# Projecting the values too ahead of the down product, with split operands stored during the up product and another preparation of the weights

## The chip, the core and the metric

The kernel runs on one core of a Trainium2 chip. The metric is the device time of the whole program in microseconds (us). Five engines run their own instruction queues: TensorE (PE: matmuls and transposes; PEld is its weight load), VectorE (DVE), ScalarE (ACT), GpSimd (POOL) and SyncE (SP), which here issues most DMA transfers. They meet only at semaphores.

## The reference

Four residual layers over x (32 sequences of 128 tokens, 256 features), all float32:

```python
x = x + L0_xattn(layernorm(x), ctx, ctx, mask)   # 16 heads of 16, no weights
x = x + L0_ffn(layernorm(x))                     # below
x = x + L1_xattn(layernorm(x), ctx, ctx)         # 16 heads of 64; q, k, v = x@Wq+bq, ctx@Wk+bk, ctx@Wv+bv
                                                 # softmax(q k / 8) v @ Wo + bo + query, then a layer norm
x = x + L1_ffn(layernorm(x))                     # route to the best of 8 experts of 1024; all experts'
                                                 # biases (relu(b1) @ W2 + b2) act on every token
# L0_ffn; qdq rounds to 16 bits by the maximum of the whole tensor, w_* to 4 bits by blocks of 32
x = qdq(x); up = qdq(x @ w_up.T); gate = qdq(x @ w_gate.T)       # 256 -> 768
o = qdq(qdq(gate * qdq_u16(sigmoid(gate))) * up); return o @ w_down.T
```

## The kernel before

Four functions, each a block with a queue written by hand for every engine, run one after another. Names of tiles begin with a_, b_, c_ and d_ after the function. `NB` is 32 sequences, `NC` 8 chunks of `CH` = 512 tokens, `NF` 6 and `ND` 2 blocks of 128 features. Products that need full precision are made of two parts of each operand: a rounded one (`high`, on ScalarE) and the difference (`low`, on VectorE or GpSimd); three of the four products of parts are summed (`PARTS`), so a block of 128x512 outputs from 256 features takes six matmuls.

`attention0` takes a step per sequence. Ahead of step 0, `weight_quantiser` brings all three weight matrices of the first feed forward through VectorE (six instructions each), TensorE (36 transposes in all) and ScalarE, and `statistics` makes the layer norm statistics of eight sequences; the others follow in steps 0 to 2, eight at a time. A block of its own before it loads the identity.

`feed_forward0` finds the maximum of y with GpSimd's all-reduce (`scale_of`, also for the maxima of up, gate, silu and inner), makes the up product and the gate product (`chunk`: 36 matmuls; ScalarE's `copy_chunk` empties the six banks of a chunk; VectorE's `quantise_up` rounds a chunk of up, and the copies of the gate product write over it), and then sigmoid and silu in 12 units of 2048 columns. Beside these, TensorE projects the keys of the second attention for all contexts: 64 blocks (`key_block`), contexts loaded by SP, rounded by ScalarE (`round_context`), their differences made on GpSimd (`split_context`), each block copied by ScalarE (`copy_keys`, three output buffers) and stored by SP (`store_keys`, 256 KB) in `keys_scratch`. `idle_sums` multiplies relu(b1) by the experts' second weights in 16 pieces, four loads of 128 KB each. SP issues these in one written order. Then `round_weights` and `rest_of_weights` split the down weights, and the down product follows with `low_inner`, the residual and the next layer norm's statistics.

`attention1` projects queries two sequences ahead and values too: `values(b, u, j)` on TensorE (12 matmuls a step), `copy_values` on VectorE with the bias bv added, and `round_context` and `split_context` for every second sequence. Keys come from `keys_scratch`, 1 MB for two sequences. Within a step the four groups of heads go: scores (PE, L1501), maxima (DVE, L1650), exponentials (ACT, L1798), division (DVE, L1661), transposes, copy, weighted values. The order on VectorE ends so:

```python
divide(b, 2)
copy_values(b, u, 0)
divide(b, 3)
add_residual(b - 1, (u + 1) % 2)
copy_values(b, u, 1)
```

`experts` sorts the tokens by expert, in tiles of 128 slots: VectorE builds which slot each token has, TensorE turns that into ids, GpSimd gathers the rows. Meanwhile GpSimd sums the experts' constants (L2075 to L2082), and VectorE makes of them what each expert's token lacks (`other`, L2340).

## Time and profile before

| | |
|---|---|
| time, median of 3 runs | 1593.12 us (1592.54 to 1595.28) |
| the profiled execution | 1594.02 us, span 1592.3 us |
| mean granted TensorE clock | 0.937 of full speed |
| busy PE, DVE, ACT, POOL | 1351.9, 1226.0, 1014.9, 435.5 us |
| moved by DMA | 134.54 MB, 84 GB/s over the span |
| attention 0, feed forward, attention 1, experts | 0 to 302, to 690, to 1281, to 1592 us |

The busy times say how much an engine did, not whether it set the pace; idle time of an engine that others wait for is what counts. DMA share is the mean busy share of the core's 16 DMA engines.

### The profile page before, as it was taken

How to read it: one execution, taken by the hardware profiler on the slowest of the kernel's cores; microseconds unless marked ns; L12 is line 12 of the kernel's file. 1: busy time of each engine (PE TensorE's matmuls, PEld its weight loads, DVE VectorE, ACT ScalarE, POOL GpSimd, SP SyncE). 2: the span in 40 equal slices, each digit the busy share in tenths (PEclk: the TensorE clock that was granted, in tenths of full speed). 3: DMA queues.
4: the chain of work that ended last, by engine and by line, in shares of the span. 5: the costliest groups of instructions: out<-in, count | busy, mean ns of one | idle time of the engine just before them, and what ended most of it. 6: DMA issues, size and time to landing. Idle time of an engine off the chain costs nothing. (4 is left out here: it accounts for less than half of the span.)

```text
span 1592.3 us, 35348 instructions
## 1 busy us (share of the span) xinstructions
PE 1351.9 (85%) x11195; PEld 1151.3 (72%) x11195; DVE 1226.0 (77%) x2165; ACT 1014.9 (64%) x2689; POOL 435.5 (27%) x663
## 2 busy tenths in 40 slices
PE   2688888599957797959999999999999729999996
PEld 2355555488833577958888888788888628999996
DVE  5777777667869788746888777777888677888886
ACT  2577888555567686626666665666666507888885
POOL 2434333100010120030222222222322243444553
PEclk8899999799978898979999999999999859999999
DMA  6511111000037364460221211131121047311110
GB/s 192 160 34 35 36 33 37 15 1 0 0 114 250 113 217 147 125 225 2 83 72 63 71 59 59 63 98 64 59 69 55 21 181 295 126 46 54 51 46 10
DMA packets 89827, 134.54 MB, mean 84 GB/s; under 512 B 11267, under 2 KB 74766, under 8 KB 84881
## 3 DMA queue, kind: packets, MB, share of 16 engines
q1 hardware_dynamic: 84752, 120.91, 22.9%
q0 software_dynamic: 4992, 12.60, 2.6%
q8 instruction: 44, 0.72, 0.2%
q14 instruction: 39, 0.31, 0.1%
HBM read 97.54 MB, written 38.67 MB: 86 GB/s over the span
## 5 line engine op out<-in xcount | busy, mean ns | idle before, releaser
L1798 ACT ACTIVATE c_w_raw<-c_ps_score,c_shift 128x128 f32<-128x128 f32 x512 | 183.7, 393 | 161.6 <-DVE c_shift L1653 153.0
L2182 PE MATMUL d_ps_hT<-d_zT,d_w_tile 128*128 128x128 f32 x1248 | 148.0, 277 | 2.3 <-DVE d_zT L2287 2.3
L2182 PEld LDWEIGHTS d_ps_hT<-d_zT,d_w_tile 128*128 128x128 f32 x1248 | 144.8, 194 | 2.9 <-DVE d_zT L2287 2.9
L2355 ACT ACTIVATE d_h<-d_ps_hT,d_b1T 128x128 f32<-128x128 f32 x312 | 88.4, 366 | 59.9 <-PE d_ps_hT L2182 59.9
L487 DVE TENSOR_REDUCE a_row_max<-a_ps_score 128x8 f32<-128x1024 f32 x64 | 78.0, 1219 | 58.5 <-PE a_ps_score L398 58.5
L2195 PE MATMUL d_ps_y<-d_w_parts,d_hT 128*128 128x256 f32 x936 | 121.5, 286 | 1.8 <-DVE d_res L2318 1.8
L1798 ACT ACTIVATION_READ_ACCUMULATOR c_w_raw<-c_ps_score,c_shift 128x1 f32 x512 | 119.0, 232 | 0.0
L1531 PE MATMUL c_ps_proj<-c_xnT,c_wq 128*128 128x256 f32 x768 | 110.1, 295 | 7.9 <-DVE c_v L1667 6.9
L2195 PEld LDWEIGHTS d_ps_y<-d_w_parts,d_hT 128*128 128x128 f32 x936 | 114.3, 191 | 2.0 <-DVE d_res L2318 2.0
L2306 DVE TENSOR_TENSOR d_w_parts<-d_w,d_w_parts 128x1024 fp32r<-128x1024 f32 x78 | 95.3, 1222 | 24.0 <-ACT d_w_parts L2367 23.1
L1554 PE MATMUL c_ps_proj<-c_wv,c_ctxT 128*128 128x512 f32 x384 | 106.3, 413 | 6.5 <-ACT c_qT L1820 3.3
L580 ACT ACTIVATE a_probT<-a_ps_probT 128x512 f32<-128x512 f32 x128 | 71.3, 625 | 57.2 <-PE a_ps_probT L409 57.2
L1531 PEld LDWEIGHTS c_ps_proj<-c_xnT,c_wq 128*128 128x128 f32 x768 | 98.4, 195 | 12.4 <-DVE c_v L1667 7.4
L1476 POOL TENSOR_TENSOR c_var_o<-c_mv_o,c_eps 128x1 f32<-128x1 f32 x32 | 6.7, 211 | 355.9 <-DVE c_mv_o L1711 355.9
L1594 PE MATMUL c_ps_aux<-c_wo,c_attnT 128*128 128x256 f32 x768 | 101.4, 288 | 1.7 <-DVE c_attnT L1686 1.7
L1594 PEld LDWEIGHTS c_ps_aux<-c_wo,c_attnT 128*128 128x128 f32 x768 | 95.6, 192 | 2.0 <-issue 1.9
L957 ACT ACTIVATE b_act<-b_ps 128x512 f32 (+1 forms) x96 | 56.6, 598 | 63.1 <-PE b_ps L876 58.4
L1661 DVE TENSOR_TENSOR c_w_raw<-c_w_raw,c_inv_sum 128x512 f32<-128x512 f32 x128 | 88.7, 693 | 4.4
L2367 ACT ACTIVATE d_w_parts<-d_w 128x1024 fp32r x78 | 79.8, 1051 | 17.0 <-PE d_ps_y L2195 16.8
L1650 DVE TENSOR_REDUCE c_row_max<-c_ps_score 128x4 f32<-128x512 f32 x128 | 87.3, 682 | 1.2 <-PE c_ps_score L1501 1.1
L1092 DVE TENSOR_REDUCE b_pmax<-b_act (+1 forms) x96 | 63.2, 683 | 32.2 <-ACT b_act L957 32.0
L1554 PEld LDWEIGHTS c_ps_proj<-c_wv,c_ctxT 128*128 128x128 f32 x384 | 68.9, 192 | 21.8 <-ACT c_qT L1820 5.9
(265 smaller groups left out, 3663.0 us busy)
## 6 DMA issues: line engine op xcount, KB each, us to landing
keys_scratch<-b_key_out SPq DMA_DIRECT2D x64, 256.0 KB, 2.5
c_kT<-keys_scratch SPq DMA_DIRECT2D x16, 1024.0 KB, 5.5
d_w<-w_in SPq DMA_DIRECT2D x16, 1024.0 KB, 10.3
b_x_space<-w_in SPq DMA_DIRECT2D x64, 128.0 KB, 2.8
zx_scratch<-c_zx SPq DMA_DIRECT2D x32, 256.0 KB, 2.3
a_x<-x_in SPq DMA_DIRECT2D x4, 1024.0 KB, 7.6
a_keys<-ctx_blocks_in SPq DMA_DIRECT2D x128, 32.0 KB, 2.1
a_v_raw<-ctx_in SPq DMA_DIRECT2D x4, 1024.0 KB, 8.5
```

Of the source, the lines that this page charges most:

```text
L487: dve.tensor_reduce(row_max[:, half, :], ps_score[:, half], AX_X, ALU.max).then_inc(max_done, 1)
L1531: last = pe.matmul(ps_proj[:, j, h * PT:(h + 1) * PT], weights[:, a, k, blk * P:(blk + 1) * P], src[:, c, k, :], start=(n == 0), stop=(n = ...
L1554: last = pe.matmul(ps_proj[:, j, :], ctxT[:, 1 - u // 2, a, k, tok], wv[:, c, k, j * BANK:(j + 1) * BANK], start=(n == 0), stop=(n == ND * ...
L1594: last = pe.matmul(ps_aux[:, 0:D], attnT[:, s, a, blk, :], wo[:, c, blk, :], start=(n == 0), stop=(n == BLKS * len(PARTS) - 1))
L1650: dve.tensor_reduce(row_max[:, n, :], ps_score[:, n % 2], AX_X, ALU.max).then_inc(max_done, 1)
L1661: dve.tensor_tensor(prob[:, n], prob[:, n], inv_sum[:, n, :].unsqueeze(2).to_broadcast([P, HB, P]), ALU.mult).then_inc(prob_ready, 1)
L1798: last = act.activation(prob[:, n, j, :], ps_score[:, n % 2, j, :], ACT.Exp, scale=float(KD) ** -0.5, bias=shift[:, n, j:j + 1], accum_out ...
L2182: last = pe.matmul(ps_hT[:, f, :], w1_tile[:, half, k, n * P:(n + 1) * P], zT[:, s, k, :], start=(k == 0), stop=(k == ND - 1))
L2195: last = pe.matmul(ps_y[:, 0:D], hT[:, s, a, f, :], w2_parts[:, half, b, n, :], start=(f == 0 and (a, b) == PARTS[0]), stop=(f == FB - 1 a ...
L2306: dve.tensor_tensor(w2_parts[:, half, 1], w2[:, e, half * FB // 2:(half + 1) * FB // 2, :], w2_parts[:, half, 0].bitcast(F32), ALU.subtrac ...
L2355: act.activation(h[:, f, :], ps_hT[:, f, :], ACT.Relu, bias=b1T[:, e, f:f + 1]).then_inc(h_ready, 1)
L2367: act.activation(w2_parts[:, half, 0], w2[:, e, half * FB // 2:(half + 1) * FB // 2, :], ACT.Copy)\
```

## The change

- *Opening.* `weight_quantiser` is gone. `attention0` loads x in parts of 2, 6, 8, 8 and 8 sequences, the identity within its block, and quantises w_up alone there; statistics go for sequences 0 and 1, 2 and 3, 4 to 7, and from then on one sequence ahead in each step (`statistics_ahead` on VectorE, `deviation_ahead` on GpSimd). w_up is turned in the last steps (12 transposes, 3 copies). Half of the first keys are loaded by ScalarE's queue.
- *The maximum of y* goes over TensorE (two transposes) and VectorE; GpSimd makes one all-reduce that nobody needs first.
- *During the up product* twelve items of 128x1024 are split: Wk in two halves, eight chunks of contexts, Wv in two halves. Each is loaded by SP, rounded by ScalarE, its difference made by VectorE, and both parts stored (1 MB) in `split_scratch`. The gate weights are quantised and turned there too. Before VectorE quantises up it waits for all these stores.
- *Before the down product* TensorE makes 64 key blocks and 64 value blocks. Their operands come ready from `split_scratch` by loads that GpSimd issues: 16 turns of eight blocks with 2 x 512 KB, and four loads of 1 MB for weights. Output buffers are five; pieces of `idle_sums` come after every third block, with one buffer; ScalarE copies four blocks after each unit of sigmoid and three after most units of silu. The down weights are quantised on VectorE among the last units and turned ahead of the last eight blocks. No engine starts the down product before all 128 blocks are done.
- *Attention 1* loads the values (512 KB for a sequence) from `values_scratch`; wv, `values`, `copy_values`, `round_context`, `split_context` are gone. bv is taken through Wo: eight matmuls of 128x256 and an addition to bo once, ahead of the steps.
- *Experts.* The constants' sums are eight matmuls and three copies on ScalarE; one of the wide VectorE instructions (`at_tile[:, :, 0]`) goes to ScalarE; the first gather is issued right after its own ids.

The diff, cut to its core:

```diff
+                load_x(0)
+                sp.dma_start(ident[:], eye).then_inc(ident_loaded, 16)
+                sp.dma_start(w_sb[:].rearrange("p (o i) -> p o i", i=D), w_up.rearrange("(o p) i -> p o i", p=P)).then_inc(w_loaded, 16)
+                load_mask(0)
+                load_first_keys(sp, 0, 0, range(0, HALF, 2))
+                load_x(1)
+                load_v(0)
+                load_first_keys(sp, 1, 1, range(HALF))
...
-                quantise_weights(dve)
-                statistics(0)
+                dve.wait_ge(x_loaded[0], 16)
+                statistics(0, 2)
+                quantise()
+                dve.wait_ge(x_loaded[1], 16)
+                statistics(2, 4)
...
+                def load_raw(k):
+                    if k >= 2:
+                        sp.wait_ge(split_ready, k - 1)
...
+                def store_split(k):
+                    sp.wait_ge(split_ready, k + 1)
+                    sp.dma_start(split_dram[k], split[:, k % 2].bitcast(F32)).then_inc(split_stored[k % 2], 16)
...
+                for n in range(ALL):
+                    store_block(n)
+                    if n % IDLE_EVERY == IDLE_EVERY - 1 and w2_pieces < 2 * FB:
+                        load_w2(w2_pieces)
+                        w2_pieces += 1
...
+                def load_contexts(first, end):
+                    for turn in range(first, end):
+                        if turn >= 2:
+                            pool.wait_ge(block_done, BLOCKS * (turn - 1))
+                        load_part(turn, 0)
+                        load_part(turn, 1)
...
+                pool.partition_all_reduce(one[:, 6, :], power[:, 0:1], P, bass.bass_isa.ReduceOp.max).then_inc(all_max, 1)
+                maximum(UP)
+                for s in range(2):
+                    pool.wait_ge(split_stored[s], 16 * ITEMS // 2)
+                load_part(0, 0)
+                pool.wait_ge(y_ready, 2 * NC)
+                load_half(WK, 0)
+                load_half(WK + 1, 1)
+                pool.wait_ge(product_done, (2 * NC - 1) * NF)
+                load_part(0, 1)
+                pool.wait_ge(product_done, 2 * NC * NF)
+                load_contexts(1, 2)
+                maximum(GATE)
+                load_contexts(2, 8)
+                maximum(SILU)
+                pool.wait_ge(block_done, KEYS - 4)
+                load_half(WV, 0)
+                load_contexts(8, 9)
+                pool.wait_ge(block_done, KEYS)
+                load_half(WV + 1, 1)
+                load_contexts(9, 14)
+                maximum(INNER)
+                load_contexts(14, 16)
...
+                def copy_block(n):
+                    act.wait_ge(block_done, n + 1)
+                    if n >= NO:
+                        act.wait_ge(block_stored[n % NO], 16 * (n // NO))
...
+                for u in range(NU):
+                    sigmoid(u)
+                    copy_blocks(done, done + 4)
+                    done += 4
...
                 scale_of(UP, pmax[:], factors[:, Y, 0, :])
                 by_gate[0] = 1
+                for s in range(2):
+                    dve.wait_ge(split_stored[s], 16 * ITEMS // 2)
                 quantise_up(0)
...
+                for u in range(NU):
+                    times_up(u, u % 2)
+                    if u >= 6:
+                        for step in range(2 * (u - 6), 2 * (u - 5)):
+                            quantise_down(step)
...
+                rest_of_weights(2, downT, down_parts)
+                dve.wait_ge(block_done, ALL)
...
+                def load_values(t, s):
+                    if inside(t, 4, NB - 1):
+                        sp.wait_ge(out_done, 2 * (t - 3))
+                    sp.dma_start(values[s].rearrange("p h w -> p (h w)"), values_dram[t]).then_inc(values_loaded[s], 16)
...
+                def bias_through_output():
+
+                    pe.wait_ge(w_loaded[1], 16)
+                    pe.wait_ge(bias_loaded, 16 * N_BIAS)
+                    for blk in range(BLKS):
+                        last = pe.matmul(ps_out[:, 0:2, :], bv[:, blk:blk + 1].to_broadcast([P, P]), w_raw[:, 1, blk * D:(blk + 1) * D],
+                                         start=(blk == 0), stop=(blk == BLKS - 1))
...
-                    if inside(b, *projects):
-                        copy_values(b, u, 0)
-                    if here:
                         divide(b, 3)
                     if back:
                         add_residual(b - 1, (u + 1) % 2)
-                    if inside(b, *projects):
-                        copy_values(b, u, 1)
...
-                pool.tensor_tensor(other[:], idle[:], b2[:], ALU.add).then_inc(summed, 1)
...
+                for e in range(NE):
+                    last = pe.matmul(sums[e], all_but[:, e:e + 1].to_broadcast([2 * NE, P]), constant_rows[:], start=True, stop=True)
```

## Rows read from the trace of the kernel before

**Rows 1.** Windows: busy us and count by engine, mean clock, DMA share, GB/s.

```profile
313.00:382.00 69.00, 69.00 (x286) 55.51 (x287) 46.76 (x61) 34.69 (x55) 0.00 (x0) 0.96 0.00 0
382.00:450.00 68.00, 67.90 (x291) 54.27 (x290) 54.04 (x69) 34.17 (x56) 0.35 (x1) 1.00 0.00 0
450.00:536.00 86.00, 53.67 (x272) 31.82 (x272) 78.12 (x43) 65.94 (x52) 14.15 (x5) 0.83 0.61 196
800.00:1200.00 400.00, 379.40 (x3412) 333.22 (x3414) 319.87 (x748) 256.64 (x1025) 104.79 (x184) 0.98 0.20 66
```

**Rows 2.** Timeline, ScalarE, first exponential of steps in attention 1: start, us, operation.

```profile
1033.93 0.42 ACT L1798 ACTIVATE c_w_raw<-c_ps_score,c_shift 128x128 f32<-128x128 f32 x1
...
1050.86 0.43 ACT L1798 ACTIVATE c_w_raw<-c_ps_score,c_shift 128x128 f32<-128x128 f32 x1
...
1068.51 0.42 ACT L1798 ACTIVATE c_w_raw<-c_ps_score,c_shift 128x128 f32<-128x128 f32 x1
...
1206.65 0.43 ACT L1798 ACTIVATE c_w_raw<-c_ps_score,c_shift 128x128 f32<-128x128 f32 x1
...
1222.20 0.43 ACT L1798 ACTIVATE c_w_raw<-c_ps_score,c_shift 128x128 f32<-128x128 f32 x1
...
1237.04 0.41 ACT L1798 ACTIVATE c_w_raw<-c_ps_score,c_shift 128x128 f32<-128x128 f32 x1
```

**Rows 3.** Timeline, VectorE, attention 0; in brackets the idle time before.

```profile
7.69 1.75 DVE L97 TENSOR_REDUCE a_w_scale<-yT 128x48 f32<-128x1536 f32 x1 [7.54 <-DMA yT<-w_up_in]
...
40.95 1.23 DVE L487 TENSOR_REDUCE a_row_max<-a_ps_score 128x8 f32<-128x1024 f32 x1 [9.01 <-PE a_ps_score L398]
...
80.86 1.23 DVE L487 TENSOR_REDUCE a_row_max<-a_ps_score 128x8 f32<-128x1024 f32 x1 [7.71 <-PE a_ps_score L398]
...
127.16 1.22 DVE L487 TENSOR_REDUCE a_row_max<-a_ps_score 128x8 f32<-128x1024 f32 x1 [1.50 <-PE a_ps_score L398]
```

**Rows 4.** Timeline, GpSimd, opening of the first feed forward.

```profile
308.40 0.38 POOL L851 PARTITION_ALL_REDUCE b_one<-b_one  x1 [5.60 <-issue]
```

**Rows 5.** Groups by line and shape, 450 to 608 us: busy, mean ns, idle before.

```profile
L1005 ACT ACTIVATE b_key_out<-b_ps,b_bk 128x512 f32<-128x512 f32 x63 | 40.6, 682 | 16.7 <-PE b_ps L901 8.4 <-DMA keys_scratch<-b_key_out 8.1
L1157 DVE SCALAR_TENSOR_TENSOR b_act<-b_act,yT 128x2048 f32<-128x2048 int32 x12 | 29.5, 2462 | 0.3 <-ACT b_act L980 0.3
...
L978 ACT ACTIVATE b_act<-yT,b_factors 128x2048 f32<-128x2048 int16 x12 | 24.0, 2000 | 4.9 <-DVE yT L1151 4.9
...
L891 PE MATMUL b_ps<-b_x_space,b_b1T 128*32 128x256 f32 x128 | 12.9, 482 | 22.5 <-DMA b_x_space<-w_in 22.5
L996 ACT ACTIVATE b_ctx_high<-b_ctx_raw 128x1024 fp32r<-128x1024 f32 x8 | 8.4, 1051 | 2.9 <-DMA b_ctx_raw<-ctx_t_in 2.9
```

**Rows 6.** Timeline, VectorE, first quantising of up.

```profile
386.96 5.28 DVE L1103 TENSOR_SCALAR b_up<-b_act,b_factors 128x3072 int16<-128x3072 f32 x3
```

**Rows 7.** DMA issues of the page: KB of each, us to landing.

```profile
keys_scratch<-b_key_out SPq DMA_DIRECT2D x64, 256.0 KB, 2.5
c_kT<-keys_scratch SPq DMA_DIRECT2D x16, 1024.0 KB, 5.5
```

**Rows 8.** Timeline, TensorE, first matmul of the down product.

```profile
616.28 0.55 PE L931 MATMUL b_ps<-b_down_high,b_inner 128*128 128x256 f32 x1 [8.43 <-DVE b_inner L1233]
```

**Rows 9.** Windows with much DMA traffic, columns as in rows 1.

```profile
500.00:505.00 5.00, 3.39 (x26) 1.60 (x25) 4.70 (x3) 4.97 (x5) 0.00 (x0) 1.00 0.83 254
1284.00:1296.00 12.00, 3.81 (x33) 3.33 (x33) 10.03 (x19) 0.00 (x0) 7.95 (x5) 0.64 1.00 418
```

**Rows 10.** Timeline, TensorE, opening of attention 1.

```profile
714.67 4.47 PE L1531 MATMUL c_ps_proj<-c_xnT,c_wq 128*128 128x256 f32 x24 [6.92 <-DVE c_v L1667]
```

**Rows 11.** Timeline, GpSimd and VectorE, opening of the experts.

```profile
1289.71 4.49 POOL L2075 TENSOR_TENSOR d_other<-d_idle,d_b 128x2048 f32<-128x2048 f32 x1 [3.97 <-DMA d_idle<-idle_scratch]
...
1289.80 4.44 DVE L2257 TENSOR_SCALAR d_slot_tile<-d_slot 128x32 int32<-128x32 int32 x1
...
1294.27 0.18 DVE L2258 TENSOR_SCALAR d_slot_row<-d_slot 128x32 int32<-128x32 int32 x1
```

880 lines of the change are left out of this document (498 added, 382 removed).

## Prediction, made before the change was run

> **What bounds the kernel now.** I read the page's slices first (TensorE busy nearly everywhere), then tables of windows by stage, then per stage the groups of lines and the timeline around each handover. The kernel is four blocks in a row, and what is last differs in each, so each part is costed in its own stage.
>
> [rows 1] show three regimes. In the two products of the first feed forward (313 to 450 us) TensorE is busy 69.0 of 69 and 67.9 of 68 us: only TensorE counts, and 291 matmuls of 512 columns in 67.9 us make 0.233 us each, thus 1.40 us for a block of six. From 450 to 536 it is busy 53.7 of 86 us: VectorE (78.1) and ScalarE (65.9) pace the stage, and the keys that TensorE projects there are its filler. In the second attention TensorE is busy 379 of 400 us, yet it isn't what sets a step: [rows 2] give the steps by their first exponential. Two neighbours take 16.93 and 17.65 us; the second is one that also splits a pair of contexts. Step 29 (1206.65) takes 15.55, step 30 (1222.20), which projects neither queries nor values, 14.84. Had TensorE set the step, the 12 value matmuls of 512 columns (2.8 us at 0.233) and the 24 of the queries less would have saved far more than 0.7. The step is a ring between ScalarE's exponentials and VectorE's maxima and divisions, and only a VectorE instruction inside that ring has a price.
>
> **The change, part by part**, against the profiled execution (1594.02, span 1592.3; the median of the runs, 1593.12, is 0.9 below it).
>
> *Opening of attention 0.* VectorE begins on the first weight matrix at 7.69 and takes the first row maximum at 40.95 [rows 3]: three matrices, statistics of eight sequences, and the turning of 36 pieces lie between. After, one matrix is quantised there: six instructions, three as wide as the first (1.75) and three lesser, which I estimate at 7 us together. Also, two sequences go first, and the identity's own block is gone, which I put at 1.5 us. I estimate load 5.5, statistics, quantiser to 12.5, two more sequences 1.1: first maximum near 14, so −27. The stall of 7.71 us at 80.86 (keys behind 3 MB of values and x) has the same cause and should stay, about 1 us shorter: −28. Bounds: −20 if keys or masks land late, −33 if that stall goes too. The per-step statistics (two instructions, 0.6 us) fit in VectorE's idle 1.50 us before each maximum [rows 3]; without that cover they would cost 24 × 0.6 = 14 us. Turning w_up in the tail: +1, since the tail waits for latencies and not for TensorE.
>
> *The maximum of y.* POOL's first all-reduce starts 5.60 us after it could [rows 4], with nothing that it waits for. It is replaced by two transposes and two short VectorE instructions (about 1.5 us in all), and a dummy all-reduce takes that delay aside: −4 (bounds −3 and −5).
>
> *During the up product.* Twelve items of 512 KB: a load, ScalarE's rounding 1.05 (the same tile in [rows 5]), VectorE's difference 1.23 (half of the 2.46 of a tile twice as wide there), a store of 1 MB; also gate's quantiser (7 us VectorE, 12 transposes, 3 copies). VectorE goes from 46.8 to 46.8 + 14.8 + 7 = 68 of 69 us, or to some 64 because the last items fall behind the product's end; ScalarE from 34.7 to about 50. The bytes, 18 MiB in 69 us, are 274 GB/s where now there are none. TensorE's work grows by some 1.5 us. The dear place is the end. VectorE waits for all split stores before it quantises up's first chunk. Before, that starts at 386.96 (5.28 for three, thus 1.8 each, [rows 6]); TensorE needs the first bank after six blocks from 382.5, thus at 391.0. After, the last two items are split at about 386.8, their stores land (a load of 1 MB took 5.5 us, [rows 7]) at about 393, VectorE 1.8, copy 0.6: 395.7, so TensorE stands about 4.5 us. With the transposes +5.5 (bounds 0, if the stores end early; +12, if the items drag behind).
>
> *From 450 to the first down matmul (616.28, [rows 8]): 166 us now.* After, TensorE does 128 blocks × 1.40 = 179, sixteen sums of pieces at 0.95 = 15 (four matmuls of 0.48 that overlap in part, and the gaps around them, [rows 5]), three groups of transposes 1.5: 195 us. It starts at once, for its first operands are loaded in the gate product. It replaces filler by work that bounds the stage: ScalarE has 128 copies × 0.68 = 87 and, for twelve units, three activations each of about the 2.00 of [rows 5], 72, in the same 195, VectorE the same as before plus 9 for the down weights; both fit. SILU's all-reduce no longer stops TensorE. But bytes: 32 MiB of blocks out, 16 MiB contexts, 4 weights and 8 w2 in, 62.9 MB. The w2 pieces all fall among the first 48 blocks: 12 + 6 + 2 + 8 MiB = 29.4 MB in what TensorE does in 82 us, 359 GB/s. Now this stage reached 254 GB/s at a DMA share of 0.83, 306 if full, while pure reads elsewhere reached 418 at 1.00 [rows 9]. By the nearer row, at about 325 GB/s, the first part takes 90 instead of 82: +8 (bounds 0 at 418, +14 at 306). The rest needs 302 GB/s: just about hidden. WV's load waits for block 60: +2. Then inner's rounding to the first down matmul, 3 us. Sum 195 + 8 + 2 + 3 = 208, so +42 (bounds +28: sums overlap and the DMA keeps up; +65: all at 272 GB/s). The down product's first matmul took 0.55 [rows 8], at the lower clock after 8 idle us; after 3 idle us it may keep the clock: −2 (bounds 0 and −3).
>
> *Opening of attention 1.* TensorE stands 6.92 us until VectorE has written values [rows 10], which is late through wo's 1 MB, its rounding and VectorE's 2.3 us. No wv, no context. But the new bias product also needs wo and all biases landed and adds 8 matmuls and an addition before the steps; the 512 KB broadcast of bv is gone. −7 (bounds −2 and −9).
>
> *Steps of attention 1.* Removed from VectorE's ring are the second value copy in 30 steps and the split of the context in 14. Step 29 against 30 prices the former at 0.71, neighbours in the loop the latter at 0.71 too [rows 2] (0.6 in the earlier steps). 30 × 0.71 + 14 × 0.63 = 30: −30. The first value copy and ScalarE's rounding of contexts lie in gaps. The 512 KB of values per step replace a 512 KB context in every second one; at 66 GB/s now [rows 1] that is free. Bounds −20 (the queries' new wait costs what the copy gave) and −58 (half way to TensorE's own time, D below).
>
> *Opening of the experts.* POOL's first sum holds 4.49 us, and a 128x32 VectorE instruction beside it takes 4.44 where the next of its size takes 0.18 [rows 11]. That delay (4.3), a smaller one beside the second sum and one of three wide VectorE instructions, which I estimate at 2.7 together, leave the path to the gather: −7 (bounds −4: the new matmuls at half clock hold the ids up; −8.5). The subtraction for the experts' biases was hidden behind the gather and is worth nothing.
>
> The sum: −28 + 1 − 4 + 5.5 + 42 − 2 − 7 − 30 − 7 = −29.5, so 1564.5 by the profile and 1564 by the median.
>
> **Rivals.** (A) *Slower: the block stores set the product stage.* ScalarE's copy n waits for store n − 5. Stores now land in 2.5 us [rows 7], but loads of 1 MB in 5.5. The stage must lose another 30 us, 0.23 a block, to undo all gains; blocks are 1.52 us apart with the sums, so that takes a store of about 5 × 1.75 = 8.8 us from copy to landing, or 265 GB/s on the whole. For it: loads of 512 KB and 1 MB beside every store, and 306 GB/s as the full share's rate [rows 9]. Against: even 306 gives 206 us for all bytes. At 250 GB/s the stage is 252 us: 1608.
> (B) *Slower too: POOL's context loads come late.* POOL issues them a turn (8 blocks, 11.2 us) ahead. In [rows 11] POOL and VectorE hold each other up. Should the two parts together wait more than 11.2 − 5.5 = 5.7 us, over two VectorE instructions of 2.46 [rows 5], TensorE stands; at 10 us a turn, 14 × 4.3 = 60: 1624. The Trainium skill (SBUF — State Buffer, "Who interferes with whom") says that descriptors of a DMA issued from GpSimd aren't written while VectorE runs in a two-port mode, and that this, not bandwidth, is what delays it. The rows of that group, [rows 11], agree that the two engines exclude each other for a whole instruction; no row here shows a load delayed so. Against B: one VectorE instruction per load is hidden.
> (C) *The splitting is not hidden in the up product.* VectorE at 68 of 69 and 274 GB/s leave no slack; with 10 to 20 us more, 1574 to 1584.
> (D) *TensorE sets the attention steps.* Its own time in a step is 0.949 × 17.3 = 16.4 us [rows 1], 13.6 without 2.8 for the values; some 26 steps × 3.6 give −94 in place of −30: 1500. Steps 29 and 30 speak against it.
> (E) *The product stage comes cheap* (+28, the DMA keeps up): 1550.
>
> **How the numbers follow.** Forecast as summed, with its own range 1555 to 1575: 0.50. E, or a like gain in attention 1: 0.20. D: 0.02. C: 0.13. A: 0.11, B: 0.04. Of A 0.03 and of C 0.01 end near the old time: faster 0.50 + 0.20 + 0.02 + 0.12 = 0.84, same 0.04, slower 0.08 + 0.04 = 0.12. What a measurement here can tell from no change is about 0.2%, 3.2 us. The range 1535 to 1590 leaves out D, and A and B in the main.
>
> **What would show it.** After, the first row maximum stands near 14 us, and the later stall stays; no 5.6 us gap ahead of the first up matmul; TensorE idle some 5 us early in the gate product; 207 us between the last gate matmul and the first down matmul, with a DMA share near 1 in its first half and TensorE above 0.9 busy; loop steps of 16.2 to 16.3 us of both parities; no VectorE instruction of 4.4 us among the experts' slots. The prediction is wrong above all if block stores show as what ScalarE waits for throughout, if TensorE waits for contexts at every eighth block, or if the steps keep their 17 us because the ring has a wait on TensorE that I haven't seen.

## The result

The change made the kernel slower: 1650.86 us, the median of four runs (1648.56 to 1655.41), against 1592.83 us before (1588.62 to 1595.28); the ratio is 1.0371, 95% interval 1.0338 to 1.0403. The forecast was 1564 with a range of 1535 to 1590, and faster than before. In the profiled executions the difference is 55.5 us of span (1647.8 against 1592.3).

Four lines of the trace after, one for each landmark: what a line's instructions did, with their count, their shortest, median and longest duration in ns, and when the first and the last began.

```profile
L995 PE MATMUL b_ps<-b_y_parts,b_gate_high x192: 390/393/767, 367.7 to 443.8; 128*128 128x512 f32 x192
...
L1089 PE MATMUL b_ps<-b_down_high,b_inner x384: 274/285/415, 703.9 to 774.4; 128*128 128x256 f32 x192
...
L1724 PE MATMUL c_ps_score<-c_kT,c_qT x1024: 271/272/580, 803.0 to 1318.9; 64*128 64x128 f32 x171
...
L2373 PE MATMUL d_ps_hT<-d_zT,d_w_tile x1248: 270/275/582, 1368.7 to 1628.0; 128*128 128x128 f32 x179
```

The same landmarks of the kernel before, from the same view, cut the time into pieces. Each piece is a difference of two starts:

| piece | before | after | change | forecast |
|---|---|---|---|---|
| start to the last row maximum of attention 0 | 288.7 | 277.0 | −11.7 | −28 |
| to the second chunk of the up product | 34.8 | 30.5 | −4.3 | −4 + 1 |
| to the end of the gate product | 125.8 | 136.3 | +10.5 | +5.5 |
| from there to the first down matmul | 167.0 | 260.1 | +93.1 | +42 |
| the down product | 71.6 | 70.5 | −1.1 | −2 |
| to the first scores of attention 1 | 34.2 | 28.6 | −5.6 | −7 |
| to its last scores | 533.4 | 515.9 | −17.5 | −30 |
| to the first tile of the experts | 58.8 | 49.8 | −9.0 | −7 |
| to the end | 278.0 | 279.1 | +1.1 | 0 |
| sum | | | +55.5 | −29.5 |

Of the 85 us between forecast and result, 51 lie in one piece, 16 in attention 0, 12 in the steps of attention 1 and 5 in the gate product. Windows of the trace after, to be read against [rows 1]: attention 0's loop, the 64 key blocks, the 64 value blocks, the loop of attention 1.

```profile
87.00:252.00 165.00, 134.78 (x1513) 89.53 (x1515) 129.89 (x240) 123.71 (x320) 73.29 (x159) 0.94 0.11 32
444.00:602.00 158.00, 114.65 (x514) 81.19 (x512) 81.82 (x54) 94.99 (x94) 11.15 (x19) 0.85 0.67 204
602.00:700.00 98.00, 93.24 (x396) 75.45 (x395) 54.45 (x39) 55.36 (x78) 8.33 (x16) 0.97 0.83 278
930.00:1267.00 337.00, 292.77 (x2712) 263.01 (x2712) 250.66 (x598) 217.47 (x880) 89.94 (x159) 0.91 0.29 93
```

The key half lasts 158 us with TensorE busy 115 of them and the DMA share at 0.67: neither engine nor bytes are at their limit. The value half, 98 us with TensorE busy 93, is close to the forecast. What the prediction priced at 90 us is the first 48 blocks with the sixteen sums; they took 133.2 us, with TensorE busy 90 of them:

```profile
444.30:577.50 133.20, 89.85 (x418) 61.31 (x416) 69.94 (x43) 78.12 (x74) 9.20 (x15) 0.84 0.70 210
```

In both loops the mean clock is below that of the kernel before: 0.94 in attention 0, where it was 1.00, and 0.91 in attention 1, where [rows 1] show 0.98.

What waited for what in the product stage, 445 to 690 us: engine, tile and line, what it waited for, us in total, times, longest.

```profile
ACT b_out L1173 <- PE b_ps L1043: 62.0, 30, 7.7
...
DVE b_act L1372 <- ACT b_act L1159: 61.5, 12, 12.9
...
PE b_ps L1018 <- DMA b_x_space<-w_in: 43.4, 10, 8.6
...
PE b_ps L1053 <- DMA b_ctx_low<-split_scratch: 4.8, 1, 4.8
...
ACT b_out L1173 <- DMA keys_scratch<-b_out: 4.6, 1, 4.6
```

TensorE waited 43.4 us for the pieces of the experts' weights, at ten of sixteen places; ScalarE and VectorE stood behind it. Of these, 4.4 us are the first piece, whose loads SP issues only after the gate product; the other 39 us are waits for a reload of the one buffer. The same wait stood already in the kernel before: 22.5 us, in the row of [rows 5] from which the prediction took the 0.48 us of these matmuls. There VectorE and ScalarE set the pace and TensorE had time to wait. For contexts it waited 4.8 us once, and ScalarE waited for key stores 4.6 us once: rivals A and B of the prediction are not what happened.

One turn of this wait in the timeline. TensorE:

```profile
489.46 0.40 PE L1043 MATMUL b_ps<-b_ctx_high,b_w_parts 128*128 128x512 f32 x1
496.52 1.08 PE L1018 MATMUL b_ps<-b_x_space,b_b1T 128*32 128x256 f32 x8 [6.66 <-DMA b_x_space<-w_in]
```

ScalarE at the same time:

```profile
487.73 2.00 ACT L1157 ACTIVATE b_act<-yT,b_factors 128x2048 f32<-128x2048 int16 x1
489.76 1.91 ACT L1159 ACTIVATE b_act<-b_act 128x2048 int32<-128x2048 f32 x1
491.58 1.25 ACT L1173 ACTIVATE b_out<-b_ps,b_bk 128x512 f32<-128x512 f32 x2
500.50 0.69 ACT L1173 ACTIVATE b_out<-b_ps,b_bk 128x512 f32<-128x512 f32 x1 [7.67 <-PE b_ps L1043]
```

and SyncE's DMA issues:

```profile
486.37 2.27 SPq L846 DMA_DIRECT2D b_x_space<-w_in  x3
489.16 1.12 SPq L853 DMA_DIRECT2D keys_scratch<-b_out  x1
497.66 1.78 SPq L846 DMA_DIRECT2D b_x_space<-w_in  x4
```

The buffer of the pieces is free once the sums before have run, at about 485.5 (they began at 484.89). SP issues the loads of the next piece from 486.37 to 489.1, since a block's store stands ahead of them, and ScalarE could copy that block only after the sigmoid that ended at 484.2. GpSimd issues two context loads of 512 KB at 487.41 and 487.95 beside them. TensorE has made its three blocks by 489.86 and gets the piece at 496.52. While it stands, no block is made; ScalarE, which comes out of the next sigmoid at 491.58, copies what there is and runs dry for 7.67 us until 500.50, so the next store and the next load (497.66) are late in turn. It is a ring of one buffer's release, SP's order behind ScalarE's copies, and a landing beside the contexts. From the first of a piece's four issues to the last arrival took 3.7 to 5.0 us for nine of the pieces and 7.1 to 10.1 us for the other seven; those seven overlap with GpSimd's loads of contexts, of the nine only one does for more than 1 us. The experiments take the first two links apart; no run moved the contexts' loads, so that link is seen in the traces and not tested.

The other places, each against its row of before. The opening of attention 0, where [rows 3] have 40.95:

```profile
8.82 1.75 DVE L533 TENSOR_REDUCE a_w_scale<-a_w 128x48 f32<-128x1536 f32 x1 [4.00 <-DMA a_w<-w_up_in]
...
17.90 1.19 DVE L459 TENSOR_REDUCE a_row_max<-a_ps_score 128x8 f32<-128x1024 f32 x1
```

The weights landed at 8.8 and not at 5.5; the first row maximum stands at 17.90 and not at 14. The opening of attention 1, where TensorE stood 6.92 us for VectorE [rows 10], now waits for the last bias:

```profile
790.96 2.47 PE L1819 MATMUL c_ps_out<-c_w_raw,c_bv 128*128 128x256 f32 x5 [4.06 <-DMA c_br<-br_in]
```

The experts' slots, where the first of these two took 4.44 us [rows 11]:

```profile
1352.70 0.18 DVE L2449 TENSOR_SCALAR d_slot_tile<-d_slot 128x32 int32<-128x32 int32 x1
...
1352.92 0.18 DVE L2450 TENSOR_SCALAR d_slot_row<-d_slot 128x32 int32<-128x32 int32 x1
```

### The profile page after: what moved, and what is told of

Its sections match the earlier page's. It is cut to its first block and busy times, and to the rows that moved or that the text cites. A ratio compares the mean times of both kernels' runs of the same rounds, so it can differ in the third digit from the quotient of the medians.

```text
span 1647.8 us, 35334 instructions
## 1 busy us (share of the span) xinstructions
PE 1389.3 (84%) x11229; PEld 1184.0 (72%) x11229; DVE 1183.1 (72%) x2102; ACT 1047.2 (64%) x2716; POOL 431.9 (26%) x735
## 5 line engine op out<-in xcount | busy, mean ns | idle before, releaser
L1754 PE MATMUL c_ps_proj<-c_xnT,c_wq 128*128 128x256 f32 x768 | 105.9, 288 | 0.0
L1724 PE MATMUL c_ps_score<-c_kT,c_qT 64*128 64x128 f32 x1024 | 92.6, 332 | 8.5 <-ACT c_w_raw L1996 6.9
L1754 PEld LDWEIGHTS c_ps_proj<-c_xnT,c_wq 128*128 128x128 f32 x768 | 94.4, 191 | 3.8 <-issue 0.2
L1724 PEld LDWEIGHTS c_ps_score<-c_kT,c_qT 64*128 64x128 f32 x1024 | 79.2, 232 | 24.8 <-ACT c_w_raw L1996 12.7
L1878 DVE RECIPROCAL c_inv_sum<-c_row_sum 128x4 f32<-128x4 f32 x128 | 22.4, 175 | 97.1 <-ACT c_w_raw L1996 97.1
L1043 PE MATMUL b_ps<-b_ctx_high,b_w_parts 128*128 128x512 f32 x256 | 91.9, 431 | 0.0
L2558 ACT ACTIVATE d_w_parts<-d_w 128x1024 fp32r x78 | 80.4, 1054 | 13.7 <-PE d_ps_y L2386 12.6
```

The lines of the kernel that those rows point to most:

```text
L1043: last = pe.matmul(ps[:, bank(n), :], w_parts[:, h, a, k, column:column + P], ctx_parts[c % 2][b][:, k, :], start=(j == 0), stop=(j == ND ...
L1724: last = pe.matmul(ps_score[:, r, j, :], qT[rows, s, blk, tok], kT[rows, s, blk, tok], start=True, stop=True)
L1754: last = pe.matmul(ps_proj[:, j, h * PT:(h + 1) * PT], weights[:, a, k, blk * P:(blk + 1) * P], src[:, c, k, :], start=(n == 0), stop=(n = ...
L2558: act.activation(w2_parts[:, half, 0], w2[:, e, half * FB // 2:(half + 1) * FB // 2, :], ACT.Copy)\
```

## Experiments

The first eleven ran once each beside one run of the kernel before (1594.44, 1592.55 and 1591.93 us in the three groups); what is said of them rests on pieces of their traces and not on a few us of the whole. How far such a piece scatters can be read from the runs in which its code is that of the change: the last row maximum of attention 0 came at 273.5 to 279.1 us (nine runs), the piece from the last gate matmul to the first down matmul took 257.8 to 266.5 us (six runs), first to last scores of attention 1 took 513.6 to 516.6 us (eleven runs).

### The product stage: who makes TensorE wait

**Loads three stores earlier in SP's order.**

```diff
                 for n in range(ALL):
+                    if (n + 3) % IDLE_EVERY == IDLE_EVERY - 1 and w2_pieces < 2 * FB:
+                        load_w2(w2_pieces)
+                        w2_pieces += 1
                     store_block(n)
-                    if n % IDLE_EVERY == IDLE_EVERY - 1 and w2_pieces < 2 * FB:
-                        load_w2(w2_pieces)
-                        w2_pieces += 1
```

> The changed kernel with one move in SP's written order: the loads of a piece of the experts' weights stand three block stores earlier, so that they wait only until TensorE has used the buffer and not also until ScalarE has copied the block before it. Same bytes, same buffers, same engine. Theory 1 (TensorE stands 43.4 us for these loads because SP reaches them late, behind stores whose copies ScalarE makes only after a sigmoid): the wait falls from 43.4 to about 15 to 20 us, the time from the last gate matmul to the first down matmul from 260 to about 230 us, the whole to about 1620. Theory 2 (the DMA engines are the limit of the key half): the same bytes take the same time, the wait moves to stores or contexts and the whole stays within 5 us of 1650.

1634.45 us. The wait fell to 30.0 us, the piece from the last gate matmul to the first down matmul from 260.1 to 243.6. The order in the queue is a third of the matter; I had expected more (a wait of 15 to 20 us, a piece of 230).

**The loads on GpSimd's queue.** `load_w2` moved there word for word, each released by TensorE's use of the buffer alone:

```diff
+                events = sorted([(IDLE_EVERY * i, 0, i) for i in range(1, 2 * FB)] + [(BLOCKS * (t - 1), 1, t) for t in range(2, 8)])
+                for _, kind, k in events:
+                    if kind == 0:
+                        load_w2(k)
+                    else:
+                        load_contexts(k, k + 1)
-                load_contexts(2, 8)
```

> The changed kernel with those loads issued by GpSimd's queue, each as soon as TensorE has used the buffer, merged by block number with the context loads that this queue already issues. Theory 1: as for the move in SP's order, 15 to 25 us of waiting left, whole about 1620 to 1630. Rival (loads issued by GpSimd are held back by VectorE's instructions): the wait stays at 40 us or grows, and the whole stays at 1650 or above, though the run with SP's earlier order gets faster.

1628.57 us, wait 25.6, piece 239.9 us. GpSimd's loads of 128 KB landed after 3.0 us (median), SP's in the other run after 2.8: VectorE doesn't hold them back by any amount that shows. What is left is 5.2 us for the first piece and 20.4 us that I put down to the single buffer: a load can start only when the last piece is used, and three blocks (4.2 us) don't cover the arrival of a piece, 4.2 to 8.3 us after its first issue in this run.

**Only one piece loaded.** All sums take the first piece, so the experts' constants come out of the wrong weights.

```diff
-                    if n % IDLE_EVERY == IDLE_EVERY - 1 and w2_pieces < 2 * FB:
-                        load_w2(w2_pieces)
-                        w2_pieces += 1
...
-                    pe.wait_ge(w2_loaded, 64 * (i + 1))
+                    if i == 0:
+                        pe.wait_ge(w2_loaded, 64)
```

> The changed kernel with only the first piece of the experts' weights loaded; all sixteen sums use it again, so the sums of the experts' constants are of the wrong weights, but TensorE does the same matmuls. It takes away 8 MB of loads and every wait for them. Theory 1: TensorE's 43.4 us of waiting are gone and most of it comes back: 1600 to 1610; the key half runs at ScalarE's pace (6.5 us for four blocks). Theory 2 (DMA bytes): 8 MB less at 250 GB/s is 33 us, about 1617, with the DMA share still above 0.85 through the key half; under theory 1 the share falls below 0.8.

1599.07 us, 51 us less than the change. Its two halves, and then its first 48 blocks with the sixteen sums:

```profile
444.00:552.00 108.00, 103.17 (x515) 74.65 (x513) 79.53 (x53) 90.16 (x90) 9.71 (x19) 0.98 0.71 219
552.00:654.00 102.00, 93.75 (x397) 75.86 (x398) 60.27 (x46) 61.32 (x85) 8.33 (x16) 0.97 0.85 282
...
444.40:529.50 85.10, 80.35 (x418) 56.42 (x416) 61.93 (x39) 70.04 (x68) 6.94 (x14) 0.98 0.71 216
```

The key half takes 107 us instead of 158. Of the 50 us between them about 39 are idle time of TensorE; the rest is its lower clock, for the same matmuls kept it busy 115 us at a mean clock of 0.85 in the change and 103 us at 0.98 here. The first part takes 85 us, where the prediction had 82 before it added anything for bytes: that estimate of TensorE's own work held. The whole piece is 210.0 us. It looks like the forecast 208, but 8 us of that sum were for the bytes of these loads, so 200 us are what to compare it with: 3 us more lie in the first part, 6 behind the sums. This run takes away the waits and 8 MB of loads together, so it doesn't say alone which of the two cost the 50 us; the DMA share of 0.67 in the change, and the next runs, which keep all bytes, do.

**Two buffers, three outputs.** The second buffer takes the space of two output buffers.

```diff
-        w2 = x_space[:, 0:4 * D].rearrange("p (e d) -> p e d", d=D)
+        w2 = x_space[:, 0:8 * D].rearrange("p (h e d) -> p h e d", h=2, d=D)
...
-                    if i >= 1:
-                        sp.wait_ge(idle_part, i)
+                    if i >= 2:
+                        sp.wait_ge(idle_part, i - 1)
```

> The changed kernel with two buffers for the pieces of the experts' weights, paid for with two of the five output buffers; SP's order as in the changed kernel but one piece ahead. Theory 1: the loads are a whole piece ahead, their wait falls below 5 us; three output buffers hold ScalarE's copies up by some us in all: whole 1605 to 1620. Rival A of the prediction (block stores set the pace): with three buffers instead of five the stage gets slower, over 1650, and ScalarE is seen to wait for stores for tens of us.

1633.02 us.

```profile
ACT b_out L1173 <- DMA keys_scratch<-b_out: 41.4, 19, 6.1
...
ACT b_out L1175 <- DMA values_scratch<-b_out: 39.4, 22, 5.8
...
PE b_ps L1018 <- DMA b_x_space<-w_in: 17.4, 6, 4.1
```

TensorE's wait for pieces fell to 17.4 (I had expected less than 5), but ScalarE now waits 81 us for its output buffers, and the value half takes 108 us. This is rival A's mechanism, brought about by three buffers; with five it stays at 17 us. The bound that I had set for it (a store must land 8.8 us late) was for five.

**Two buffers and five outputs.** The second buffer lies where the raw down weights were; these are loaded after the last sum.

```diff
-        w2 = x_space[:, 0:4 * D].rearrange("p (e d) -> p e d", d=D)
+        w2 = [flat[:, 0:4 * D].rearrange("p (e d) -> p e d", d=D) for flat in (x_space, downT[:].rearrange("p k n -> p (k n)"))]
```

> The changed kernel with two buffers for the pieces of the experts' weights and all five output buffers: the second buffer lies where the raw down weights lay, which are loaded after the last piece instead. The run with three output buffers lost its gain again to waits for stores, most of it in the value half (108 us instead of 93). Theory 1: with both, TensorE's wait for pieces stays below 10 us of 43, the value half is 93 us again, the first down matmul comes at 660 to 670 instead of 703.9, whole 1608 to 1618. Rival (bytes: 29.4 MB within the first 48 blocks at 235 to 250 GB/s are 118 to 125 us): the key half stays at 125 us or more, first down matmul at 672 or later, whole 1620 or more.

1618.1 us, piece 223.6: the wait for pieces is 14.7 us (8.0 and 6.7 for the two buffers), 5.1 of them for the first; the key half takes 122 us at a DMA share of 0.87 and 265 GB/s. With all bytes kept, 36 of the 50 us are back. Here the expectation's two theories meet: most of the ring's wait is gone, and what is left of the loss in the key half goes with the DMA's load; no run separates that rest further. The first 48 blocks take 99 us, still more than the 96 of the prediction's upper bound. The stores, too, now land after 5.2 us instead of 3.6.

**Pieces after every fifth block**, so that they reach into the value half:

```diff
-        IDLE_EVERY = 3
+        IDLE_EVERY = 5
...
-                copy_idle()
                 copy_blocks(done, done + 3)
...
+                    if u == 7:
+                        copy_idle()
```

> The run with two buffers for the experts' weights and five output buffers, with the pieces after every fifth block instead of every third, thus over 80 of the 128 blocks; the copy and the store of the sums, and the load of the down weights, come later by 32 blocks. Theory (in the key half the engines wait for latencies of a full DMA queue; the value half has room): the key half falls from 121 to 108 to 112 us, the value half grows by the six pieces that it gets (6 to 8 us), first down matmul at 662 to 668 instead of 669.8, whole 1611 to 1617. Rival (the down weights, which now come late, hold the end up): the time from the last value block to the first down matmul grows above 6 us, whole 1618 or more.

1605.27 us, better than the theory had it; piece 216.5.

```profile
446.00:560.00 114.00, 105.96 (x508) 77.89 (x507) 89.95 (x57) 93.44 (x93) 12.57 (x22) 0.97 0.96 300
560.00:665.00 105.00, 93.93 (x422) 74.30 (x421) 52.53 (x44) 58.47 (x83) 6.76 (x13) 0.96 0.80 264
```

The halves don't part where these windows do: the last key block ends at 548.0 and the first value block starts at 553.0. The key half is down to 102 us, the value half up to 106 (it holds four pieces, and VectorE waits 15.2 us for the sums' store before it may quantise the down weights).

### Attention 0: the step of 7.62 us

**Statistics in the first steps**, as before the change; the new opening stays.

```diff
                     if b == 0:
                         statistics(4, 8)
+                    else:
+                        dve.wait_ge(x_loaded[b + 1], 16)
+                        statistics(8 * b, 8 * b + 8)
...
-                        statistics_ahead(UN * i + u, u)
```

> The changed kernel, but with the layer norm statistics of the sequences 8 to 31 made eight at a time in steps 1 to 3 of attention 0, as the kernel before has them; nothing of them in the later steps, on VectorE or GpSimd. The new opening stays. Theory (the two statistics instructions per step outgrow VectorE's gap, which lengthens the step by 0.3 us, and TensorE, idle that much longer, is granted half its clock in every third step): the steps return to 7.62 us at a clock of 1.00; 24 steps of mean 8.3 become 7.62, minus 16 us, plus what the first steps take back, about 4: the last row maximum 12 to 13 us earlier than 277.0, whole 1637 to 1640. Rival (the new opening itself or the keys' queues slow all steps): steps stay at 7.9 and 9.5, whole 1650 or more.

Of the nineteen steps of the changed kernel from 86.5 to 245.0 us, five take 7.62 us and eight 7.9 at the full clock, and six take 9.5 at a mean of 0.82. Two of them that follow each other, cut at their first row maxima; in the second TensorE is busy 1.65 us longer with as many matmuls:

```profile
152.39:160.31 7.92, 6.30 (x77) 4.32 (x78) 6.63 (x12) 6.22 (x16) 3.71 (x9) 1.00 0.10 31
...
160.31:169.88 9.57, 7.95 (x77) 4.95 (x78) 6.65 (x12) 6.22 (x16) 5.28 (x12) 0.82 0.09 29
```

The run with the statistics first took 1641.67 us. The loop's steps are 7.62 us, the clock is 1.00, the last row maximum 12.6 us earlier:

```profile
87.00:252.00 165.00, 137.07 (x1664) 94.29 (x1656) 123.96 (x217) 132.01 (x349) 65.33 (x131) 1.00 0.12 35
```

**GpSimd's part alone left in the steps.** GpSimd makes the deviation ahead in every step from statistics that VectorE made early.

```diff
-                    pool.wait_ge(mv0_done, b + 5)
-                    pool.tensor_tensor(var_next[:, u:u + 1], mv_next[:, u, 1:2], eps[:], ALU.add)
+                    pool.wait_ge(mv0_done, NB)
+                    pool.tensor_tensor(var_next[:, u:u + 1], mv0[:, b + 4, 1:2], eps[:], ALU.add)
```

> As the run with the statistics in the first steps, but GpSimd still makes the deviation of one sequence ahead in each step. If VectorE's two instructions are the cause, the steps stay at 7.62 us with the clock at 1.00 and the whole equals that run's. If GpSimd's two instructions are (they hold shared work between the queries and the values), the steps stay at 7.9 and more, and the whole is 10 us or more above that run's.

1645.58 us, and the steps are 7.93 us again, some 9.5. The last row maximum comes 9.3 us later than in the run before; the whole is only 3.9 us longer, where I had expected 10 or more, since the product stage happened to take 4.7 us less. The theory that VectorE's instructions did it fell here: they are not in this kernel's steps. GpSimd's scaling of the next queries (L288) and VectorE's shift of the row maxima (L463), in this run:

```profile
150.30 0.61 POOL L288 TENSOR_TENSOR a_q_in<-a_q_in,a_rstd_next 128x256 f32<-128x256 f32 x1
...
150.33 0.61 DVE L463 TENSOR_SCALAR a_shift<-a_row_max 128x8 f32<-128x8 f32 x1
```

and in the run with the statistics first, in another step:

```profile
149.12 0.61 POOL L288 TENSOR_TENSOR a_q_in<-a_q_in,a_rstd 128x256 f32<-128x256 f32 x1 [0.17 <-POOL a_q_in L285]
...
149.89 0.17 DVE L463 TENSOR_SCALAR a_shift<-a_row_max 128x8 f32<-128x8 f32 x1
```

GpSimd's two new instructions push its L288 past 150.3, where VectorE's shift begins; the two start 30 ns apart, and 0.17 us become 0.61. The Trainium skill (SBUF — State Buffer, "Who interferes with whom") states that GpSimd and a VectorE instruction in a two-port mode exclude each other for a whole instruction. These rows agree, as far as they go: the shift ends with L288, at 150.9. Which mode the shift is in they don't show. In the changed kernel this shift took 0.56 to 0.62 us in each of the fourteen steps of 7.87 us or more named above, and 0.17 us in each of the five of 7.62.

**The deviation in GpSimd's gap.**

```diff
                         residual(b - 2, s)
+                        if inside(b, 5, NB - 4):
+                            deviation_ahead(b - 1, (u - 1) % UN)
                         inverse_deviation(b - 2, s)
-                    if inside(b, 4, NB - 5):
-                        deviation_ahead(b, u)
```

> The changed kernel; in attention 0 GpSimd makes the deviation of the sequence ahead one step later and in its idle 3 us after the residual, instead of between the inverse deviation and the values. Work and waits are otherwise the same, and VectorE keeps both statistics instructions per step. Theory (revised by the last two runs: GpSimd's 0.7 us push its scaling of the next queries to 150.30 us, onto VectorE's shift of 128x8, which then takes 0.61 instead of 0.17 us and lengthens the step from 7.62 to 7.93; at that length TensorE's clock falls in every third step): the shift takes 0.17 to 0.37 us again, steps are 7.62 us, the clock from 87 to 252 us is 1.00 and the last row maximum comes at 262 to 266 us instead of 277.0; whole 1636 to 1640. Rival (the statistics on VectorE lengthen the steps as well): steps stay above 7.8.

1635.23 us. L288 is past before the shift comes, with all of the work still in the steps:

```profile
140.19 0.61 POOL L288 TENSOR_TENSOR a_q_in<-a_q_in,a_rstd_next 128x256 f32<-128x256 f32 x1
...
141.06 0.17 DVE L463 TENSOR_SCALAR a_shift<-a_row_max 128x8 f32<-128x8 f32 x1
```

```profile
87.00:252.00 165.00, 136.26 (x1650) 93.58 (x1648) 136.49 (x259) 133.32 (x351) 78.78 (x170) 1.00 0.12 35
```

Steps are 7.63 us, the last row maximum starts about 263 instead of 277.0, and the clock is 1.00. Of these 14 us about 4 are the longer shifts themselves (fourteen steps, 0.3 us each) and about 10 the clock (six steps, 1.6 us each). Why 0.3 us more in a step brings the clock down, no run tells. VectorE's two instructions, 0.6 us a step, do hide in its gap of 1.50 us: 0.76 are left.

### Attention 1: the clock

Two neighbouring steps of the loop after the change, cut at their first exponentials:

```profile
1132.80:1150.37 17.57, 15.34 (x134) 13.74 (x132) 12.76 (x31) 10.97 (x45) 4.63 (x9) 0.81 0.36 119
1150.37:1166.85 16.48, 14.06 (x142) 12.47 (x141) 12.57 (x31) 10.74 (x44) 4.55 (x9) 1.00 0.22 64
```

The step with the clock at 0.81 takes 17.57 us, that at the full clock 16.48.

**Matmuls without use where the value matmuls were.** Nothing reads them.

```diff
+                def fill(b, j):
+                    if inside(b, *projects):
+                        pe.wait_ge(q_ready, 4 * (b + 2) + 2 * (j + 1))
+                        for m in range(6):
+                            pe.matmul(ps_proj[:, j, :], wq[:, 0, m % ND, 0:P], wq[:, 0, m % ND, j * BANK:(j + 1) * BANK],
+                                      start=True, stop=True)
```

> The changed kernel with 12 matmuls of 512 columns without use in each step of attention 1, where the value matmuls were (same waits, nothing reads them). VectorE and ScalarE do no more than in the changed kernel. Theory (TensorE is granted a lower clock since it has less to do: 0.91 against 0.97 in the loop, and steps that should take 16.3 to 16.5 take 17.0 in two of three): the clock returns to about 0.97, most loop steps take 16.3 to 16.5, attention 1 is 6 to 10 us shorter, whole about 1642. Rival (the steps are longer for a wait on loads or on the new order, not for the clock): no gain, or up to 10 us more because TensorE's 2.8 us per step are added on its path.

1644.77 us. In the loop:

```profile
930.00:1267.00 337.00, 327.43 (x3028) 288.68 (x3027) 254.59 (x611) 220.88 (x896) 92.90 (x164) 1.00 0.29 93
```

More work on TensorE, and each step of the loop takes 16.48 to 16.64 us, where without it they take 16.48 to 17.57. First to last scores are 505.7 us instead of 515.9: 10.2 us, at the clock of 1.00. The whole gained only 5 us: the first scores come 9 us later than in the changed kernel, but the fill in the two steps ahead of step 0 accounts for 4.8 of them (from the last down matmul, 33.4 us instead of 28.6). The product stage, whose code is the same, took 6.4 us longer, and attention 0, with the same code too, 2.6 us less.

### The gate product

After the change, ScalarE's last rounding in the up stage, and TensorE's wait in the gate product's second chunk:

```profile
374.57 1.06 ACT L1127 ACTIVATE b_split<-b_split_raw 128x1024 fp32r<-128x1024 f32 x1 [2.85 <-DMA b_split_raw<-wv_in]
```

```profile
383.65 1.19 PE L995 MATMUL b_ps<-b_y_parts,b_gate_high 128*128 128x512 f32 x2 [7.38 <-ACT b_act L1115]
```

**Items earlier**, none after the last chunk:

```diff
-            return (range(0, 1), range(1, 2), range(2, 3), range(3, 5), range(5, 7), range(7, 8), range(8, 10), range(10, 12))[c]
+            return (range(0, 1), range(1, 2), range(2, 3), range(3, 5), range(5, 7), range(7, 9), range(9, 12), range(0))[c]
```

> The changed kernel with the last four items of the splitting spread over chunks 5 and 6 of the up product (two and three items), none after chunk 7. Theory: the split stores end 4 us or more before VectorE wants to quantise up, so TensorE's wait for the first bank of the gate product falls from 7.38 to below 2 us and the whole gets 4 to 7 us faster (1643 to 1646). Rival C of the prediction (loads, not the place of the items, are late: the last raw item landed only 8 us after its issue): VectorE and ScalarE wait for the same loads inside the up product, the up product gets as much longer as the gate product gets shorter, whole 1650.

1646.14 us, but the gate product ends at 442.0 instead of 443.8, and half of that is attention 0, which ended 0.9 us earlier. The gate product is 7.5 us shorter and the up product as much longer: the wait was moved, not removed. TensorE now stands 6.4 us ahead of the first gate block:

```profile
ACT b_split L1127 <- DMA b_split_raw<-wv_in: 7.8, 2, 4.7
...
PE b_ps L995 <- ACT b_act L1115: 7.5, 2, 6.4
```

The raw items land late wherever they stand (ScalarE waits 7.8 us for Wv's two). Rival C of the prediction describes this, but at 5 us and not at 10 to 20. Which part of SP's alternation of stores and loads makes them late wasn't tried.

### All repairs at once

The edits of two buffers with five outputs, every fifth block, the deviation in the gap and the fill together; the fill starts at step 0 instead of two steps ahead of it, and the raw down weights come after the last sum:

```diff
-                sp.dma_start(downT[:].rearrange("p k n -> p (k n)").rearrange("p (o i) -> p o i", i=FF),
-                             w_down.rearrange("(o p) i -> p o i", p=P)).then_inc(down_loaded, 16)
...
-                    if n == KEYS:
+                    if n == IDLE_EVERY * 2 * FB:
...
+                        sp.dma_start(downT[:].rearrange("p k n -> p (k n)").rearrange("p (o i) -> p o i", i=FF),
+                                     w_down.rearrange("(o p) i -> p o i", p=P)).then_inc(down_loaded, 16)
...
+                    if inside(b, 0, NB - 3):
```

> The changed kernel with the three repairs together: pieces of the experts' weights in two buffers and after every fifth block, the deviation in GpSimd's gap, and the twelve matmuls without use per step of attention 1, these now only from step 0 on (in the two steps before it they held the opening up by 9 us). If the three places are independent, the gains measured one by one add up: 1605 by the first, minus 14 by the second, minus 10 by the third (515.9 us from the first to the last scores became 505.7), thus 1578 to 1586, faster than the kernel before by 0.4 to 1.0%. Rival (a shared cause: an earlier stage that ends sooner only shifts the clock's falls into the next): one or two of the gains don't show and the whole stays at 1590 or more.

1582.92 us, median of five (1581.71 to 1585.24), against 1590.99 before: ratio 0.9947, interval 0.9934 to 0.9961. It is 0.5% faster than the kernel before, clear of noise, and 4% faster than the changed one. Both loops run at the full clock:

```profile
87.00:252.00 165.00, 136.49 (x1650) 93.51 (x1648) 136.56 (x260) 133.28 (x352) 78.57 (x170) 1.00 0.12 35
900.00:1200.00 300.00, 291.38 (x2691) 257.35 (x2690) 226.78 (x546) 197.64 (x804) 81.72 (x144) 1.00 0.29 94
```

Its pieces: 221.4 us from the gate product to the first down matmul, 505.2 from the first to the last scores, the last row maximum at 263.0. The gains add up. Against the kernel before this is −25.7 us to the last row maximum (forecast −28), −28.2 in the steps of attention 1 (forecast −30) and +54.4 in the product stage (forecast +42): the first two forecasts could be had once their loops ran at the full clock, the third was too low even without the ring.

## Why the prediction was wrong, point by point

- **From 450 to the first down matmul** is the step that failed: "at about 325 GB/s, the first part takes 90 instead of 82: +8". It took 133 us. I priced this part by bytes, and the DMA never came near that rate there (210 GB/s at a share of 0.70). What set it were 43.4 us of waiting for pieces in a single buffer whose loads stood behind ScalarE's copies in SP's order, and the lower clock of TensorE behind each wait. The run with one piece has the same matmuls and takes 85 us for this part; the run with two buffers and all bytes takes 99. I had looked for the ring only at the outputs (rival A) and at the contexts (rival B), though the row of [rows 5] that I cited for these matmuls has 22.5 us of the same wait. TensorE's own work, 82 us, held. So of the 51 us that this stage is off, 43 are here and 8 behind the sums (126 us instead of 118), where the change of weights had 2 us in the sum and cost 4.8. That the run with one piece gives 210 us, close to the 208 of the sum, is in part luck: its bytes term no longer applied.
- **Opening of attention 0**: −28 forecast, −11.7 measured. 4 us of it are the first row maximum at 17.90 instead of 14, since the weights landed later. 14 us are the step; smaller gains in the rest take 2 us off again. That the statistics fit in VectorE's idle 1.50 us held for VectorE. I had not priced GpSimd's two instructions at all, nor what they collide with: a shift in time of 0.7 us on an engine with 3 us of idle time. Shown by moving them into that idle time: −14.
- **The clock** was missing from both loops. A step that grew from 7.62 to 7.93 us was granted half the clock for a part of every third step or so, which then took 9.5; a loop that lost 2.8 us of matmuls a step fell to a mean of 0.91. In attention 1 that ate 10 of the 30 us, shown by the fill. The chain itself was priced almost right: 16.5 us a step, forecast 16.2 to 16.3. (The neighbours that priced it are 0.72 us apart and not 0.71, which changes nothing.)
- **The maximum of y** (−4) and **the down product** (−2) came in, the one as −4.3 together with the tail's +1, the other as −1.1. **Opening of attention 1**: −5.6 for −7; it waits 4.06 us for the biases and then makes the bias product at a mean clock of 0.69, in 5.2 us; the wait for the biases was in the forecast's working, the lower clock only in that of the experts. **Experts**: −9.0 for −7. The 4.44 us are gone, and also the 2 us beside the second sum (a cast of 128x32 took 2.20 us before and 0.18 after).
- **The gate product**: +10.5 for +5.5, by the late raw items. The mechanism (all stores before quantising up) was right, the size wasn't: TensorE stands 7.38 us in place of 4.5. (393 + 1.8 + 0.6 makes 395.4 and not 395.7, which is no part of it.)
- D and E did not come. A and B did not set the pace with five output buffers: ScalarE waited 17 us in all for stores, TensorE 4.8 us once for contexts.

## What to carry to other kernels

Price a stage by its rings, not only by its busy engines and its bytes: for each buffer that is reused, follow the load from the event that frees it, through every queue in which the load stands behind something else, to its use, and compare that with the work in between. One buffer with 4.2 us of cover for pieces that took 4 to 10 us to arrive cost most of 50 us here; a second one, in space that was free for just that time, gave 32 us of the whole back. Read the idle time of a row too when you take its duration, also where that idle time costs nothing yet. Moving work onto an idle engine has a price if it shifts that engine's other instructions: look at what they will start beside.

## What the runs showed of the hardware

- Taking work off TensorE can lengthen a loop that it doesn't bound: 12 useless matmuls of 512 columns a step raised the mean granted clock from 0.91 to 1.00 and shortened the steps from a mean of about 16.9 to 16.5 us. The means mix the clock's two levels, 1.2 and 2.4 GHz; TensorE was busy 87% of the loop where its clock fell in some steps, and 97% in the loop with the fill, where it stayed at 2.4. The Trainium skill (TensorE: Matmul & The Clock Gate, "HAM oscillation — how this bites in real kernels") describes a throttle that comes and goes with the gaps in a kernel's matmuls. The runs agree in that the full clock came back when the gaps were filled; but the page's case has waits of several us for DMA, and here no idle time of TensorE in the loop was longer than 1.2 us (0.5 with the fill).
- A VectorE instruction on 128x8 elements took 0.61 us instead of 0.17 when it started 30 ns after a GpSimd one of 0.61 us; both ended together.
- GpSimd-issued loads of 128 KB landed in 3.0 us (median) in a stage where VectorE was busy 61% of the time, against 2.8 us from SP.
